# Layer norms of a four-layer graph network: squares by ScalarE in two halves of the tiles, and two elementwise steps of the last norm taken elsewhere

## The chip, the cores and the metric

One NeuronCore of a Trainium2 chip runs the whole network in one launch. The metric is device time in microseconds (us), the median over runs. TensorE is called PE in the profile, VectorE DVE, ScalarE ACT, GpSimd POOL and SyncE SP; they run unsynchronized, each through its own instruction stream, and meet at semaphores.

## The reference, cut to what matters

There are 3125 nodes with 128 features and 50000 edges. Each of the four layers takes the layer norm of x, clips it at zero, runs one graph layer on it and adds the result to x. The last layer (graph attention with 4 heads) ends in a layer norm of its own, with scale and shift:

```python
def _layernorm(x, axis=-1, eps=1e-05):
    m = jnp.mean(x, axis=axis, keepdims=True)
    v = jnp.var(x, axis=axis, keepdims=True)
    return (x - m) / jnp.sqrt(v + eps)

# layer 3 (attention), the end
combined = h_self + h_in.reshape(n, -1) + h_out.reshape(n, -1) + bias
mean = combined.mean(axis=-1, keepdims=True)
var = combined.var(axis=-1, keepdims=True)
normed = (combined - mean) * jax.lax.rsqrt(var + EPS_LN)
return normed * ln_gamma + ln_beta

# the frame around the four layers
h = jnp.maximum(_layernorm(x, axis=-1), 0.0)
x = x + _L0_gnn_ref(h, ...)
...
h = jnp.maximum(_layernorm(x, axis=-1), 0.0)
x = x + _L3_gnn_ref(h, ...)
```

## The kernel before, in words

**Tiling.** Nodes lie on the 128 partitions, in 25 tiles: `x`, `h` and `comb` (a view of `rdeg`) are 128 x 25 x 128 in f32, so a pass over all nodes is one instruction of 3200 elements a partition. `scr` is a view of the same size in `arena`.

**Stages.** First the edges are sorted and a dense matrix A of edge counts is built (up to about 850 us). Layers 0 to 2 each multiply the normed features by A (`dense_pe`, and `wide_pe` for the second step of layer 1) and then by weights. Layer 3 writes a table of projected rows to memory, GpSimd gathers 50000 padded edge rows from it (`stream_pool`), and in two directions d the kernel finds maxima (`top_*`), exponents (`guard_*`) and weighted sums (`weighted_*`). The last norm and the store of x end the program.

**The norms.** Norm 0 is GpSimd's (`first_norm`) and isn't touched. Norms 1, 2 and 3 stand ahead of layers 1, 2 and 3; norm 4 is the one that ends layer 3. They are `norm_dve(v, n, relu)`, L901 to L915. On DVE, one after the other: sum of each row (L904), mean (L905), subtraction of the mean (L906), square (L907), sum of the squares (L908). Then ScalarE takes the root (`norm_act`, L948) and DVE the reciprocal (L910) and the product (L912, or L915 in norm 4). `dve_link` adds a semaphore wait of DVE on its own last instruction. Nothing else of the layer runs meanwhile: PE waits for `h`. In norms 1 and 2 the split of `h` into three 16-bit parts (`split_dve`, `split_act`) stands between the norm and PE's product with A.

**The last norm.** Ahead of norm 4 DVE copies `comb` to `h` (L1605), and behind it stand the product with gamma (L1607), the addition of beta (L1608) and the addition to x (L1609), which releases the store.

**What sets the order.** Every engine's stream is in the order of the code; there is no scheduler. ScalarE's tables are loaded by an instruction that the compiler puts ahead of the first function that needs another set.

**Start of the attention.** DVE writes `h` for the table (L1571), then `comb` (L1573), then the indices that GpSimd waits for (L1577 to L1579), then digits and one-hot figures (L1580 to L1595, L1127, L1131). GpSimd's first gather waits for the indices and for both tables in memory.

Of the kernel before, what the change touches and what calls it, by code (L numbers as in the profile page):

```python
# [10 lines left out]
ALU = mybir.AluOpType  # L11
ACT = mybir.ActivationFunctionType
AX_X = mybir.AxisListType.X

P = 128
N_NODES, N_EDGES, D = 3125, 50000, 128
TILES = -(-N_NODES // P)
# [67 lines left out]
ROW = {"fc3": 0, "L2_self": 1, "L2_nei": 2, "L3_bias": 3, "gamma": 4, "beta": 5}  # L85
# [3 lines left out]
def linker(eng, sem):  # L89

    count = [0]

    def link(ins):
        count[0] += 1
        ins.then_inc(sem, 1)
        eng.wait_ge(sem, count[0])

    return link


def gnn_kernel(nc, edges, x_in, consts, steps, weights, bias_cols, bias_rows, attn, out):
    with ExitStack() as ctx:
        def sb(name, shape, dt=F32):
            return ctx.enter_context(nc.sbuf_tensor(name, shape, dt))

        def sem(name):
            return ctx.enter_context(nc.semaphore(name))
# [20 lines left out]
        brow = sb("brow", [P, ROWS, D])  # L128
# [5 lines left out]
        x = sb("x", [P, TILES, D])  # L134
        h = sb("h", [P, TILES, D])
        rdeg = sb("rdeg", [P, NP_])
        st = sb("st", [P, 8, TILES])
# [30 lines left out]
        scr = aggT.rearrange("p (t f) -> p t f", t=TILES)  # L168
# [72 lines left out]
        comb = rdeg[:, :].rearrange("p (t f) -> p t f", t=TILES)  # L241
# [52 lines left out]

        table = {n: sem(f"table_{n}") for n in ("att0", "att1")}
        digits_ready = sem("digits_ready")
        round_done = sem("round_done")
        scatters_begun = sem("scatters_begun")

        var_ready, std_ready, rstd_ready = sem("var_ready"), sem("std_ready"), sem("rstd_ready")  # L300
# [36 lines left out]
        dve_link = linker(nc.vector, dve_step)  # L337
# [432 lines left out]
        def split_need(t, n):  # L770
            def ready(k):
                for g, (c0, _) in enumerate(SPLITS):
                    if k == c0:
                        t.wait_ge(lo_ready, 1 + SPLIT_FROM[n] + g + 1)
            return ready
# [11 lines left out]
        def spread_src_dve(v):  # L787

            v.tensor_copy(spread, bc(src_deg[:, :], P)).then_inc(src_spread, 1)
            for m in range(DEG_PIECES):  # L790
                c = deg_piece(m)
                v.wait_ge(src_turned, m + 1)
                v.tensor_copy(rdeg[:, c], PS[:, SORT:SORT + c.stop - c.start]).then_inc(src_read, 1)
            v.wait_ge(src_read, DEG_PIECES)
# [39 lines left out]
        def h1_split_act(a):  # L834
            def hi(n):
                bank, _, p = h1_of(n)
                a.wait_ge(h1_turned, n + 1)
                a.copy(p[0], bank).then_inc(hi_ready, 1)

            def mid(n):  # L840
                _, left, p = h1_of(n)
                a.wait_ge(mid_rest, H1_MID + n + 1)
                a.copy(p[1], left).then_inc(mid_ready, 1)

            for n in range(TURNS + 1):
                if n < TURNS:
                    hi(n)
                if n:
                    mid(n - 1)
# [39 lines left out]
        def wide_dve(v):  # L889
            for b in range(BANDS):  # L890
                v.wait_ge(half_used, (b + 1) * TILES)
                for c in range(2):
# [2 lines left out]
                    v.tensor_tensor(agg2T[:, c, n].rearrange("p (q n) -> p q n", q=BQ), slot(c),  # L895
                                    rdeg[:, n].rearrange("p (q n) -> p q n", q=BQ), ALU.mult).then_inc(agg_ready, 1)

        def bc(a, n):
            return a.unsqueeze(2).to_broadcast([P, a.shape[1], n])

        def norm_dve(v, n, relu):  # L901

            src = x if relu else h
            dve_link(v.tensor_reduce(st[:, 0, :], src[:, :, :], AX_X, ALU.add))  # L904
            dve_link(v.tensor_scalar(st[:, 0, :], st[:, 0, :], 1.0 / D, None, ALU.mult))  # L905
            dve_link(v.tensor_tensor(h[:, :, :], src[:, :, :], bc(st[:, 0, :], D), ALU.subtract))  # L906
            dve_link(v.tensor_tensor(scr, h[:, :, :], h[:, :, :], ALU.mult))  # L907
            v.tensor_reduce(st[:, 1, :], scr, AX_X, ALU.add).then_inc(var_ready, 1)  # L908
            v.wait_ge(std_ready, n + 1)
            dve_link(v.reciprocal(st[:, 3, :], st[:, 2, :]))  # L910
            if relu:
                v.scalar_tensor_tensor(h[:, :, :], h[:, :, :], 0.0, bc(st[:, 3, :], D), ALU.max, ALU.mult) \  # L912
                    .then_inc(h_ready, 1)
            else:
                dve_link(v.tensor_tensor(h[:, :, :], h[:, :, :], bc(st[:, 3, :], D), ALU.mult))  # L915
# [28 lines left out]
            p.tensor_tensor(narrow[2], left, narrow[1], ALU.subtract).then_inc(lo_ready, 1)  # L944

        def norm_act(a, n):
            a.wait_ge(var_ready, n + 1)
            a.activation(st[:, 2, :], st[:, 1, :], ACT.Sqrt, bias=eps[:, 0:1], scale=1.0 / D).then_inc(std_ready, 1)  # L948

# [458 lines left out]
        def weighted_out_dve(v, d):  # L1408
            v.wait_ge(weighted_done, d + 1)
            n = TILES * HEADS  # L1410
            den = rden[:, 0, :]
            dve_link(v.tensor_reduce(den.rearrange("p (t h) -> p t h", h=HEADS), PS[:, DEG_COL:DEG_COL + SPLIT * n]
                                     .rearrange("p (t s h) -> p t h s", s=SPLIT, h=HEADS), AX_X, ALU.add))
            dve_link(v.tensor_scalar(den, den, 1e-8, None, ALU.add))
            dve_link(v.reciprocal(rden[:, 1, :], den))
            hv = h[:, :, :].rearrange("p t (h f) -> p (t h) f", h=HEADS)
            dve_link(v.tensor_tensor(hv, PS[:, 0:NP_].rearrange("p (n f) -> p n f", f=HD),
                                     rden[:, 1, :].unsqueeze(2).to_broadcast([P, n, HD]), ALU.mult))
            dve_link(v.tensor_tensor(comb, comb, h[:, :, :], ALU.add))
            v.nop().then_inc(den_ready, 1)  # L1420
# [65 lines left out]
        def _(v):  # L1486
# [21 lines left out]
            def row(a):  # L1508
                return a.unsqueeze(1).to_broadcast([P, TILES, D])
# [16 lines left out]
            dve_link(v.tensor_tensor(x[:, :, :], x[:, :, :], h[:, :, :], ALU.add))  # L1526

            norm_dve(v, 1, True)
            split_dve(v, 1)
            count_src_dve(v)  # L1530
# [10 lines left out]
            dve_link(v.tensor_tensor(x[:, :, :], x[:, :, :], h[:, :, :], ALU.add))  # L1541

            norm_dve(v, 2, True)
            split_dve(v, 2)
            spread_src_dve(v)
# [3 lines left out]
            dve_link(v.scalar_tensor_tensor(x[:, :, :], h[:, :, :], 0.0, x[:, :, :], ALU.max, ALU.add))  # L1549

            norm_dve(v, 3, True)
            v.wait_ge(hT_ready, HT_DONE + 1)
            v.wait_ge(score_summed, 1)
# [23 lines left out]
            dve_link(v.tensor_scalar(k0, back_i, 255, None, ALU.bitwise_and))  # L1577
            dve_link(v.tensor_scalar(key[:, 0, 0:CH[0]], k0, -1.0, None, ALU.add))
            v.tensor_scalar(k0, back_i, 8, None, ALU.arith_shift_right).then_inc(order0_ready, 1)  # L1579
            v.tensor_copy(figures, iota[:, 0:BASE])  # L1580
            for d in range(2):
                whole = digit_i[:, 0, 0:CH[d]]
# [16 lines left out]
            for d in range(2):  # L1599
# [2 lines left out]
                guard_dve(v, d)  # L1602
                weighted_dve(v, d)
                weighted_out_dve(v, d)
            dve_link(v.tensor_copy(h[:, :, :], comb))  # L1605
            norm_dve(v, 4, False)
            dve_link(v.tensor_tensor(h[:, :, :], h[:, :, :], row(brow[:, ROW["gamma"], :]), ALU.mult))  # L1607
            dve_link(v.tensor_tensor(h[:, :, :], h[:, :, :], row(brow[:, ROW["beta"], :]), ALU.add))  # L1608
            v.tensor_tensor(x[:, :, :], x[:, :, :], h[:, :, :], ALU.add).then_inc(x_final, 1)  # L1609

        @block.tensor
# [114 lines left out]
        def _(a):  # L1726
            a.wait_ge(wx_summed, 1)
            a.copy(Wx[:, :], PS[:, 6 * BANK:6 * BANK + SC]).then_inc(wx_ready, 1)
            norm_act(a, 0)
            a.wait_ge(placed, 1)  # L1730
            permute_act(a)
# [7 lines left out]
            a.wait_ge(sumsq_ready, 1)  # L1739
            a.activation(st[:, 7, :], st[:, 6, :], ACT.Sqrt).then_inc(len_ready, 1)  # L1740
            norm_act(a, 1)
            split_act(a, 1)
            ht_act(a, 1)
# [5 lines left out]
            act_link(a.activation(scr, scr, ACT.Exp, scale=-1.0))  # L1749
            a.activation(scr, scr, ACT.Ln, bias=1.0).then_inc(log_ready, 1)  # L1750
            norm_act(a, 2)
            split_act(a, 2)
            ht_act(a, 2)
# [85 lines left out]
```

## Time and profile before

| | us |
|---|---|
| median of 3 runs | 3366.75 |
| lowest, highest | 3361.63, 3368.27 |
| the profiled execution's own time | 3377.51 |
| its span, first to last instruction | 3375.7 |
| DVE busy in the span | 2277.1 (67%) |
| ACT busy | 835.0 (25%) |
| PE busy | 2190.7 (65%) |
| POOL busy | 1657.2 (49%) |

Time outside the span is 1.8 us. Busy shares are means over stages that different engines bound. In the four norms only DVE works for the layer; GpSimd still scatters sorted edges beside norms 1 and 2.

### The profile page before, as it was taken

To read this page: it belongs to the slowest core of one execution; us is meant where nothing else is said; L and a number is where in the kernel's file an instruction comes from. 1 tells how busy PE (TensorE), PEld (TensorE's weight loads), DVE (VectorE), ACT (ScalarE), POOL (GpSimd) and SP (SyncE) were. 2 spreads that over 40 slices of the span, in tenths; PEclk is the share of its full clock that TensorE was granted. 3 is DMA by queue.
4 is the path that set the end of the run, shared out by engine and by line. 5 is a ranking of instruction groups with operands and counts; after the bars stand their busy time and mean duration, and the time that the engine had idled before them with its cause. 6 is when DMAs were issued, how large, how long until landed. Compare 5 with 4: busy or idle time off the path is not lost.

```text
span 3375.7 us, 46741 instructions
## 1 busy us (share of the span) xinstructions
PE 2190.7 (65%) x12603; PEld 1296.6 (38%) x12659; DVE 2277.1 (67%) x3122; ACT 835.0 (25%) x1389; POOL 1657.2 (49%) x1455
## 2 busy tenths in 40 slices
PE   0488877777895989994963444434566665528562
PEld 0233455554452455542442111111456611118562
DVE  8999888898549720055132544444986799979777
ACT  0099433332001110022000111111344322206341
POOL 7400133332057777777104777777876777710000
PEclk9799999999997999997975555565569999955897
DMA  2000011110443524400725434435358733530452
GB/s 71 0 0 0 30 44 44 44 44 34 159 124 98 147 65 99 84 1 1 170 45 97 115 111 111 117 110 108 85 165 264 233 111 110 98 33 0 150 177 74
DMA packets 195115, 301.52 MB, mean 89 GB/s; under 512 B 120540, under 2 KB 133818, under 8 KB 194922
## 3 DMA queue, kind: packets, MB, share of 16 engines
q1 hardware_dynamic: 138986, 175.88, 16.7%
q0 software_dynamic: 40512, 62.87, 10.8%
q10 hardware_dynamic: 15552, 61.94, 6.0%
q8 instruction: 36, 0.59, 0.1%
q14 instruction: 29, 0.24, 0.0%
HBM read 191.65 MB, written 88.01 MB: 83 GB/s over the span
## 4 chain that ended last, share of the span: by engine, by line
PE 35%; POOL 19%; DVE 17%; issue 17%; DMA 6%; ACT 5%; ACTq 1%; DVEq 0%; SPq 0%; POOLq 0%; PEldq 0%
POOL arena L1304 19%; PE PS L537 11%; PE PS L698 9%; PE PS L883 6%; DMA arena<-T_att,idx 5%; ACT arena L513 4%; DVE arena L558 4%; PE PS L972 3%; PE PS L475 2%; PE PS L959 1%; DVE arena L1195 1%; DVE arena L373 1%; DVE arena L489 1%; DVE arena L566 1%; DMA T_att<-parts 1%
## 5 line engine op out<-in xcount | busy, mean ns | idle before, releaser
L1304 POOL DMA_INDIRECT arena<-T_att,idx x864 | 845.9, 979 | 323.1 <-issue 229.1
L537 PE MATMUL PS<-arena 128*128 128x400 f16 (+2 forms) x4320 | 780.6, 332 | 270.4 <-issue 112.1
L1139 DVE TENSOR_REDUCE arena<-PS 128x1024 f32 (+1 forms) x432 | 502.6, 1212 | 334.3 <-PE PS L1106 334.0
L537 PEld LDWEIGHTS PS<-arena 128*128 128x128 f16 (+2 forms) x4320 | 528.2, 158 | 513.6 <-issue 350.9
L1477 POOL DMA_INDIRECT order<-arena x400 | 514.2, 1285 | 249.4 <-issue 249.4
L558 DVE TENSOR_SCALAR arena<-arena 128x1600 f16<-128x1600 f16 x448 | 392.3, 919 | 63.1 <-PE PS L537 59.0
L1106 PE MATMUL PS<-arena,pick 128*128 128x512 bf16 x812 | 319.1, 493 | 154.1 <-DVE arena L1139 140.2
L698 PE MATMUL PS<-arena 128*128 128x512 f16 (+1 forms) x1575 | 318.1, 361 | 95.4 <-issue 82.1
L632 POOL TENSOR_TENSOR rdeg<-rdeg,arena 128x1600 f32<-128x1600 f32 x48 | 160.7, 3348 | 311.8 <-ACT arena L616 311.8
L1095 PE MATMUL PS<-ident_b,score_buf 128*32 128x128 bf16 x864 | 90.4, 268 | 314.8 <-ACT score_buf L1068 305.2
L698 PEld LDWEIGHTS PS<-arena 128*128 128x128 bf16 x1575 | 147.9, 99 | 261.6 <-issue 110.2
L1095 PEld LDWEIGHTS PS<-ident_b,score_buf 128*32 128x32 bf16 x864 | 66.9, 119 | 380.5 <-issue 305.2
L513 ACT ACTIVATE arena<-arena 125x128 f16<-125x128 f16 x600 | 186.1, 388 | 77.4 <-DVE arena L492 72.0
L1106 PEld LDWEIGHTS PS<-arena,pick 128*128 128x128 bf16 x864 | 61.9, 108 | 364.3 <-DVE arena L1139 319.8
L1351 DVE TENSOR_TENSOR arena<-PS,key 128x1024 f32<-128x1024 f32 x108 | 132.2, 1224 | 88.6 <-PE PS L537 86.2
L1241 PE MATMUL PS<-ident_b,arena 128*128 128x128 bf16 x864 | 109.4, 306 | 87.1 <-issue 66.5
L616 ACT CAST arena<-PS 128x1600 f16<-128x1600 f32 x50 | 74.6, 1492 | 345.1 <-PE PS L537 344.9
L1074 ACT COPY arena<-PS 32x1024 bf16<-32x1024 bf16 x108 | 107.8, 999 | 192.5 <-PE PS L1095 188.9
L883 PE MATMUL PS<-arena 128*128 128x400 f16 x800 | 147.1, 338 | 10.8 <-DVE arena L860 8.8
L972 PE MATMUL PS<-arena,W 128*128 (+1 forms) x384 | 136.7, 515 | 20.9 <-DVE arena L1002 10.2
L1273 ACT COPY arena<-PS 128x1024 bf16<-128x1024 bf16 x108 | 109.3, 1012 | 161.0 <-PE PS L1241 160.5
L1068 ACT COPY score_buf<-h 128x96 bf16 (+1 forms) x52 | 14.1, 271 | 535.1 <-POOL h L1313 535.1
(258 smaller groups left out, 2781.0 us busy)
## 6 DMA issues: line engine op xcount, KB each, us to landing
spill<-arena SPq DMA_DIRECT2D x108, 560.0 KB, 2.9
arena<-spill ACTq DMA_DIRECT2D x108, 560.0 KB, 3.8
arena<-A SPq DMA_DIRECT2D x50, 800.0 KB, 4.6
A<-arena SPq DMA_DIRECT2D x50, 400.0 KB, 2.4
arena<-A SPq DMA_DIRECT2D x50, 400.0 KB, 3.3
arena<-T_att,idx POOLq DMA_INDIRECT x864, 2.6
order<-arena POOLq DMA_INDIRECT x400
T_att<-h SPq DMA_DIRECT2D x2, 1600.0 KB, 13.9
```

What stands on the lines that cost most here:

```text
L513: last = a.activation(B0[:, g, j, k, :], eq0[:, g, j, :], ACT.Copy, scale=sort_v[:, 2 + k, c])
L537: return t.matmul(where, lhsT, rhs, start=False, stop=True, skip_group_check=True)
L558: v.tensor_scalar(oh_d[s], steps_h, dst_in[:, bass.ds(RING_D * i + s, 1)], None, ALU.is_equal) \
L632: p.tensor_tensor(at, at, stage[c % RING_A], ALU.add).then_inc(cell_counted, 1)
L698: last = t.matmul(PS[:, a0:a1], narrow[s][:, k, :], strips[g % RING][:, a0:a1], start=(k == 0 and s == 0), stop=(k == TILES - 1 and s == S ...
L883: last = t.matmul(PS[:, at:at + w], wide[c][s][:, k, :], halves[n % HALVES][:, q * w:(q + 1) * w], start=(k == 0 and s == 0), stop=(k == T ...
L972: last = t.matmul(o, wt(name, c * H1 + ob * P), rhs, start=(n == 0), stop=(n == len(terms) - 1))
L1095: last = t.transpose(bank[:, j * P:(j + 1) * P], score_buf[:, half, j, :], ident_b[:, :])
L1106: last = t.matmul(PS[:, hd * BANK:(hd + 1) * BANK], pick[:, hd, :], sT[:, s:s + QUAD, :].rearrange("p j e -> p (j e)"), start=True, stop=True)
L1139: v.tensor_reduce(cmax[d][:, u:u + 2, bass.ds(i * SLOTS + half * GROUP + q // 2 * QUAD, QUAD)], PS[:, u * BANK:(u + 2) * BANK].rearrange(" ...
L1304: p.indirect_dma_start(out=ring1[:, b, j, :], out_offset=None, in_=T_att[d][:, :], in_offset=bass.IndirectOffsetOnAxis(ap=idx[:, d, k:k + ...
L1477: p.indirect_dma_start(out=order0[:, :], out_offset=bass.IndirectOffsetOnAxis(ap=addr[:, j:j + 1], axis=0), in_=packed[:, j:j + 1], in_off ...
```

## The change

`norm_dve` subtracts the mean in two instructions, of 13 and of 12 tiles (`PARTS_T`), each of which increments `centred`. ScalarE waits for each and writes its squares to `scr` (increment of `squared`). DVE waits for each and sums it; the sum over a part is an instruction of its own, and the last increments `var_ready`. Norm 4 reads `comb` itself, so the copy to `h` goes. The addition of beta to x stands behind the indices at the start of the attention, and the one to `h` at the end goes.

```diff
@@ norm_dve
-            src = x if relu else h
+            src = x if relu else comb
             dve_link(v.tensor_reduce(st[:, 0, :], src[:, :, :], AX_X, ALU.add))
             dve_link(v.tensor_scalar(st[:, 0, :], st[:, 0, :], 1.0 / D, None, ALU.mult))
-            dve_link(v.tensor_tensor(h[:, :, :], src[:, :, :], bc(st[:, 0, :], D), ALU.subtract))
-            dve_link(v.tensor_tensor(scr, h[:, :, :], h[:, :, :], ALU.mult))
-            v.tensor_reduce(st[:, 1, :], scr, AX_X, ALU.add).then_inc(var_ready, 1)
+            for t in PARTS_T:
+                v.tensor_tensor(h[:, t, :], src[:, t, :], bc(st[:, 0, t], D), ALU.subtract).then_inc(centred, 1)
+            for k, t in enumerate(PARTS_T):
+                v.wait_ge(squared, 2 * (n - 1) + k + 1)
+                last = v.tensor_reduce(st[:, 1, t], scr[:, t, :], AX_X, ALU.add)
+            last.then_inc(var_ready, 1)
@@ norm_act
+            for k, t in enumerate(PARTS_T if n else ()):
+                a.wait_ge(centred, 2 * (n - 1) + k + 1)
+                a.activation(scr[:, t, :], h[:, t, :], ACT.Square).then_inc(squared, 1)
             a.wait_ge(var_ready, n + 1)
@@ start of the attention, behind the indices
+            v.tensor_tensor(x[:, :, :], x[:, :, :], row(brow[:, ROW["beta"], :]), ALU.add)
             v.tensor_copy(figures, iota[:, 0:BASE])
@@ the end
-            dve_link(v.tensor_copy(h[:, :, :], comb))
             norm_dve(v, 4, False)
             dve_link(v.tensor_tensor(h[:, :, :], h[:, :, :], row(brow[:, ROW["gamma"], :]), ALU.mult))
-            dve_link(v.tensor_tensor(h[:, :, :], h[:, :, :], row(brow[:, ROW["beta"], :]), ALU.add))
```

DVE's stream in norm 1, before and then after (`arena` is `scr` here):

```order
L904 TENSOR_REDUCE st<-x 128x25
L905 TENSOR_SCALAR st<-st 128x25
L906 TENSOR_TENSOR h<-x,st 128x3200
L907 TENSOR_TENSOR arena<-h 128x3200
L908 TENSOR_REDUCE st<-arena 128x25
L910 RECIPROCAL st<-st 128x25
```

```order
L907 TENSOR_REDUCE st<-x 128x25
L908 TENSOR_SCALAR st<-st 128x25
L910 TENSOR_TENSOR h<-x,st 128x1664
L910 TENSOR_TENSOR h<-x,st 128x1536
L913 TENSOR_REDUCE st<-arena 128x13
L913 TENSOR_REDUCE st<-arena 128x12
L916 RECIPROCAL st<-st 128x25
```

The square has left DVE, and the subtraction and the sum of squares are two instructions each. Lines of the changed kernel are some lines further down than those of before.

ScalarE's stream around norm 2, before and then after: absolute value, exponential and logarithm of layer 1's end, then the norm.

```order
L1749 ACTIVATE arena<-arena 128x3200
L1750 ACT_TABLE_LOAD
L1750 ACTIVATE arena<-arena 128x3200
L948 ACT_TABLE_LOAD
L948 ACTIVATE st<-st,eps 128x25
```

```order
L1757 ACTIVATE arena<-arena 128x3200
L1758 ACT_TABLE_LOAD
L1758 ACTIVATE arena<-arena 128x3200
L955 ACTIVATE arena<-h 128x1664
L955 ACTIVATE arena<-h 128x1536
L957 ACT_TABLE_LOAD
L957 ACTIVATE st<-st,eps 128x25
```

No load stands ahead of the squares; the root's load now comes behind them, here and in norm 4. In norms 1 and 3 no load is added.

DVE's stream at the start of the attention, after the change:

```order
L1588 TENSOR_SCALAR idx<-arena 128x416
L1589 TENSOR_TENSOR x<-x,brow 128x3200
L1590 CAST W<-cst 128x8
```

The middle row is new: x plus beta, behind the last instruction that GpSimd's gathers wait for.

## Rows read from the trace of the kernel before

**Rows 1.** The page: span, busy time by engine, the chain by engine.

```profile
span 3375.7 us, 46741 instructions
PE 2190.7 (65%) x12603; PEld 1296.6 (38%) x12659; DVE 2277.1 (67%) x3122; ACT 835.0 (25%) x1389; POOL 1657.2 (49%) x1455
PE 35%; POOL 19%; DVE 17%; issue 17%; DMA 6%; ACT 5%; ACTq 1%; DVEq 0%; SPq 0%; POOLq 0%; PEldq 0%
```

**Rows 2.** Timeline, norm 1: start us, length us, engine, line, [idle before <-releaser].

```profile
1024.19 3.49 DVE L904 TENSOR_REDUCE st<-x 128x25 f32<-128x3200 f32 x1
...
1028.21 3.49 DVE L906 TENSOR_TENSOR h<-x,st 128x3200 f32<-128x3200 f32 x1
...
1031.74 3.49 DVE L907 TENSOR_TENSOR arena<-h 128x3200 f32<-128x3200 f32 x1
...
1035.27 3.48 DVE L908 TENSOR_REDUCE st<-arena 128x25 f32<-128x3200 f32 x1
...
1038.79 0.32 ACT L948 ACTIVATE st<-st,eps 128x25 f32<-128x25 f32 x1 [22.24 <-DVE st L908]
1039.14 0.31 DVE L910 RECIPROCAL st<-st 128x25 f32<-128x25 f32 x1 [0.38 <-ACT st L948]
...
1047.75 6.57 PE L698 MATMUL PS<-arena 128*128 128x512 f16 x21 [37.91 <-issue]
```

**Rows 3.** Timeline, ScalarE from layer 1's end through norm 2.

```profile
1569.20 1.28 ACT L1750 ACT_TABLE_LOAD   x1
1570.49 2.87 ACT L1750 ACTIVATE arena<-arena 128x3200 f32<-128x3200 f32 x1
1573.38 1.28 ACT L948 ACT_TABLE_LOAD   x1
...
1595.04 0.32 ACT L948 ACTIVATE st<-st,eps 128x25 f32<-128x25 f32 x1 [20.38 <-DVE st L908]
```

**Rows 4.** Timeline, PE's first work behind norm 3.

```profile
1755.81 4.54 PE L952 MATMUL PS<-cst,h 128*128 128x128 f32 x25 [25.64 <-DVE h L912]
```

**Rows 5.** Timeline, smaller pieces in the split behind norm 1.

```profile
1044.09 2.36 DVE L754 TENSOR_TENSOR arena<-h,arena 128x1024 f32<-128x1024 f32 x2 [1.11 <-ACT arena L734]
...
1046.29 1.15 ACT L734 CAST arena<-h 128x1152 bf16<-128x1152 f32 x1
...
1047.56 1.35 DVE L754 TENSOR_TENSOR arena<-h,arena 128x1152 f32<-128x1152 f32 x1
```

**Rows 6.** Timeline, start of the attention: DVE's preparations, the first gather, the first consumer.

```profile
1798.03 0.38 DVE L1579 TENSOR_SCALAR idx<-arena 128x416 int32<-128x416 int32 x1
...
1805.39 0.18 DVE L1131 TENSOR_TENSOR score_buf<-W 128x32 bf16<-128x32 bf16 x1
1813.13 1.01 POOL L1304 DMA_INDIRECT arena<-T_att,idx  x1 [37.09 <-DMA T_att<-parts]
...
1833.24 0.27 ACT L1068 COPY score_buf<-h 128x96 bf16<-128x96 bf16 x1 [70.03 <-POOL h L1313]
```

**Rows 7.** Timeline, the program's end.

```profile
3323.78 1.28 ACT L948 ACT_TABLE_LOAD   x1
...
3335.94 1.83 DVE L1605 COPY h<-rdeg 128x3200 f32<-128x3200 f32 x1
...
3359.85 3.49 DVE L1608 TENSOR_TENSOR h<-h,brow 128x3200 f32<-128x3200 f32 x1
3363.38 3.49 DVE L1609 TENSOR_TENSOR x<-x,h 128x3200 f32<-128x3200 f32 x1
3366.90 0.41 SPq L1456 DMA_DIRECT2D out<-x  x1
```

**Rows 8.** Timeline, PE in two successive rounds of the last weighted sums.

```profile
3175.57 2.05 PE L537 MATMUL PS<-arena 128*128 128x128 f32 x16 [0.96 <-issue]
...
3178.71 2.05 PE L537 MATMUL PS<-arena 128*128 128x128 f32 x16 [0.91 <-issue]
```

**Rows 9.** Windows: stretch, its us, busy us of five engines, PE's granted clock, DMA.

```profile
3170.00:3180.00 10.00, 6.87 (x76) 6.57 (x75) 7.21 (x7) 4.58 (x8) 0.00 (x0) 1.00 0.58 177
```

More of the change, by code:

```diff
@@ L296, in gnn_kernel @@
         digits_ready = sem("digits_ready")
+        centred, squared, senders_summed = sem("centred"), sem("squared"), sem("senders_summed")
         round_done = sem("round_done")
@@ L896, in wide_dve @@
                                     rdeg[:, n].rearrange("p (q n) -> p q n", q=BQ), ALU.mult).then_inc(agg_ready, 1)
+        PARTS_T = (slice(0, TILES // 2 + 1), slice(TILES // 2 + 1, TILES))
         def bc(a, n):
```

## The prediction

> **What bounds the kernel now.** I first read the page: DVE is busy 67% of the span and PE 65%, and the chain that ended last is PE 35%, GpSimd 19%, DVE 17% [rows 1]. No engine bounds the whole, so a change is worth what it is worth in its own stage. Then the timeline of a norm. In norm 1 DVE runs one full-size instruction after the other, each starting 0.03 to 0.04 us after the last (1028.21 + 3.49, then 1031.74); PE stands idle and starts only at 1047.75, after 37.91 us [rows 2]. Norm 2 stands alone in the same way: ScalarE had been idle 20.38 us when the sum of squares released it [rows 3]. In norm 3 PE, idle for 25.64 us, is released by DVE's product L912 directly [rows 4]. At the end nothing runs but DVE, and the store is issued 0.03 us after its last addition [rows 7]. So all four norms lie on the path, DVE alone makes them, and the time of each is a sum of its instructions.
>
> GpSimd also works beside norms 1 and 2 (the scatters of the sort), but nothing waits for it there: its first gather waits for the table in memory [rows 6].
>
> **The cost of the smaller instructions.** The trace shows no DVE pass over 13 or 12 tiles (1664 or 1536 elements a partition). It has 3.49 us for 3200 elements [rows 2] and 1.35 us for 1152 [rows 5]: 1.045 ns an element and 0.15 us fixed. That gives 1.89 us for 13 tiles and 1.75 for 12. The same line is taken for the sums, since L908 with 3.48 costs what L907 does. Two instructions that don't wait for each other overlap by 0.07 us: a pass of 1024 is 1.22 by that line, and two together took 2.36 [rows 5].
>
> ScalarE's square from `h` to `scr` isn't shown either. The nearest rows are its logarithm over the same 3200 elements, 2.87 us [rows 3], and its cast of 1152 from `h`, 1.15 us [rows 5]: 0.84 ns an element and 0.18 fixed. So 1.58 us for 13 tiles and 1.47 for 12.
>
> A handoff from DVE to ScalarE costs 0.04 us: L908 ends at 1038.75, the root starts at 1038.79. Back it costs 0.03: the root ends at 1039.11, the reciprocal starts at 1039.14 [rows 2].
>
> **Part 1, the squares, four times.** Before, from the start of the subtraction to the start of the root: 1038.79 - 1028.21 = 10.58 us [rows 2]. After, with the subtraction of the first part at 0:
> - first subtraction ends at 1.89, the second runs from 1.82 to 3.57;
> - first square from 1.93 to 3.51, beside the second subtraction; second square from 3.61 to 5.08;
> - first sum from 3.60 (DVE is free at 3.57, its square was done at 3.51) to 5.49; second sum from 5.42 to 7.17, its square long done;
> - root at 7.21.
>
> That is 3.37 us a norm: the whole square (3.53 with its gap) less the second fixed cost of two DVE passes, part of which the overlap returns. Neither square is on the path; what hides the second is the first sum, with 0.34 us to spare (5.42 against 5.08). Four norms give 13.5 us. The bounds: at best the square goes and nothing comes, 3.53 a norm, 14.1. At worst neither overlap happens (0.14) and each of DVE's two waits for a square costs 0.38, the whole idle time that DVE shows around the root [rows 2], although 0.32 of it was the root itself: 3.37 - 0.14 - 0.76 = 2.5 a norm, 10 in all. I take 13.5, near the upper end, since two of the rows (the handoffs of 0.04 and 0.03) are the very kind of wait that is added.
>
> Queued behind DVE's two waits are only the norm's own later steps. On ScalarE nothing else stands there: in norms 1 and 2 the casts that need the finished `h`, in norm 3 the copy behind PE's transposes.
>
> **The root's table.** Before norms 2 and 4 ScalarE loads the root's table while idle (1573.38, and 3323.78 during the last weighted sums) [rows 3, 7]. Now the load follows the second square: from 5.08 to 6.37, and the root isn't wanted until 7.21. The second sum hides it with 0.84 us to spare. Were that cover gone, it would cost its 1.28.
>
> The trace shows a switch at 1.29 us from the start of the load to the start of the logarithm, with 0.02 us ahead of it [rows 3]. The Trainium skill, "ScalarE: Activation LUTs", section "What ACT_TABLE_LOAD costs", puts a drain of about 1380 ns on top, 2.66 us for every switch. By that rule, an estimate from the page, the root would be ready at about 7.74 and norms 2 and 4 would each lose 0.5 us; the trace doesn't agree with it, so my sum leaves it out.
>
> **Part 2, the copy ahead of norm 4.** It goes with its gap: 1.83 + 0.03 = 1.86 us [rows 7]. The sum L904 and the subtraction then read `comb`, an f32 tile of the same size in the same memory, so they keep 3.49. Bounds 1.8 and 1.9.
>
> **Part 3, beta.** At the end one addition with its gap goes: 3363.38 - 3359.85 = 3.53 us [rows 7]. At the start of the attention the same instruction is added behind the indices (1798.03 + 0.38 = 1798.41). It pushes DVE's remaining preparations back by 3.5 us, from an end at 1805.57 to 1809.1. The first gather waits for the table, until 1813.13, and not for DVE; the first consumer of the figures comes with ScalarE's copy at 1833.24 [rows 6]. The cover is 24 us, so I cost it at 0; without it the price would be the 3.5 us. GpSimd issues nothing in that stretch for DVE to disturb.
>
> **The sum.** 13.5 + 1.86 + 3.53 = 18.9 us. The profiled execution took 3377.51 (3375.7 of span and 1.8 around it), so its like would take 3358.6. The median shown is 10.8 us under the profiled execution; the terms don't depend on that difference, and 3366.75 - 18.9 = 3347.9. I predict 3348.
>
> **Rivals.**
> 1. *Only the tail is kept.* What norms 1 to 3 give (10.1 us) is absorbed at a gate that doesn't move with them: a strip of A not yet landed, or the gather stage. Then 3.37 + 1.86 + 3.53 = 8.8 us remain, 3358. The same total, near enough, comes if the squares take twice as long beside a busy DVE: second square done at 8.1 instead of 5.1, 0.8 us gained a norm, 8.6 in all. For the gate: gathers wait on memory. Against it: behind norms 1 and 2 the product starts when the split is done, and the gathers start when the table lands, which is itself released by DVE's and PE's chain from norm 3. Against slow squares: ScalarE's 1152-element cast had DVE beside it and lies on the same line as the lone 2.87.
> 2. *Beta isn't free.* DVE's preparations hold somebody. Then 15.4 us, 3351.4. Against it the 24 us of cover.
> 3. *The switch with its drain.* The root's table is ready only at about 7.7, because the load can't follow a busy ScalarE at once. From a ready time 0.5 us late in two norms the gain is 17.9, 3348.9. For it: here the load stands behind a square, with the root wanted soon after. Against it: in norm 2 the present load began 0.02 us after the logarithm and ended 1.29 later. The page that states this is named above.
> 4. *Slower: PE loses its clock in the last weighted sums.* Everything reaches that stage earlier than before by 10 us, and the granted clock there could come late. The granted clock is 1.00 (2.4 GHz) in this stretch [rows 9], a round takes 3.14 us, and its 16 matmuls 2.05 [rows 8]. At half the clock these would be some 4.1 (an estimate, twice 2.05), so a round would lengthen by 2.05. Of its 56 rounds 9 at half clock cancel the gain, and 13 make the kernel slower by over 0.2%; all 56 would cost 115 us. Against it: the work that comes before the stage is the same instruction by instruction, and the three runs shown lie within 6.6 us.
>
> That the change doesn't do what it says I leave without a chance of its own: the streams show the square gone from DVE.
>
> **Chances.** Forecast (16 to 21 us gained) 0.78; drain 0.04; beta not free 0.05; only the tail or slow squares 0.09; PE's clock 0.04. A measurement of this kernel tells about 0.2% (6.7 us) from no change. The first three are faster beyond that (0.87), of the fourth two thirds (0.06, the rest falls within as its 8.8 us is near the bound), and the clock case is slower with 0.03 and within with 0.01. Faster 0.93, same 0.04, slower 0.03.
>
> The range: the sum's own bounds are 10 + 1.8 + 3.53 = 15.3 and 14.1 + 1.9 + 3.53 = 19.5, so 3347 to 3351; the runs of before lie from 5 us under to 1.5 above their median, and a new set of runs has the same spread. The fourth case ends at 3358. I take 3340 to 3358.
>
> **What would show it.** In norms 1 to 4: subtractions of about 1.89 and 1.75 us, squares of 1.58 and 1.47 on ScalarE, the root 7.2 us after the first subtraction's start instead of 10.6. DVE idle ahead of the first sum for about 0.03 us and ahead of the second for none. In norms 2 and 4 a load of 1.28 us that ends before the second sum. DVE's last preparation of the attention 3.5 us later against the table's write, and the first gather still released by the table. From the last addition to comb to the store's issue 31.0 - 3.4 - 1.9 - 3.5 = 22.2 us (before: 3366.90 - 3335.94 = 31.0). What would prove me wrong: a wait of DVE on `squared` of over 0.3 us, full-size passes that got longer, or a stage between 1060 and 3320 that changed its length by more than some 3 us.

## The result, and the profile after

The changed kernel takes 3346.68 us (median of 5 runs, 3344.86 to 3349.36), the kernel before 3366.34 in the same comparison (5 runs, 3361.63 to 3368.27). The ratio is 0.9947, 95% interval 0.9937 to 0.9958: 19.7 us less. The forecast was 3348, 18.9 less.

The page of the changed kernel, beside [rows 1] (its profiled execution took 3349.36 us):

```profile
span 3347.6 us, 46752 instructions
PE 2186.4 (65%) x12603; PEld 1297.7 (39%) x12659; DVE 2262.1 (68%) x3125; ACT 846.9 (25%) x1397; POOL 1645.1 (49%) x1455
PE 35%; POOL 19%; issue 16%; DVE 16%; DMA 6%; ACT 5%; ACTq 1%; DVEq 0%; SPq 0%; POOLq 0%; PEldq 0%
```

DVE has 15 us less work and ScalarE 12 more: in each of the four norms the two squares of 1.59 and 1.48 us. The shares hardly tell of the change. The timeline of norm 1 does (start us, length us, engine, line, [idle before <-releaser]; lines are those of the changed kernel), against [rows 2]:

```profile
1023.72 3.49 DVE L907 TENSOR_REDUCE st<-x 128x25 f32<-128x3200 f32 x1
...
1027.74 3.56 DVE L910 TENSOR_TENSOR h<-x,st 128x1664 f32<-128x1664 f32 x2
1029.66 3.15 ACT L955 ACTIVATE arena<-h 128x1664 f32<-128x1664 f32 x2 [13.59 <-DVE h L910]
1031.29 3.54 DVE L913 TENSOR_REDUCE st<-arena 128x13 f32<-128x1664 f32 x2
1034.87 0.32 ACT L957 ACTIVATE st<-st,eps 128x25 f32<-128x25 f32 x1 [2.05 <-DVE st L913]
1035.21 0.31 DVE L916 RECIPROCAL st<-st 128x25 f32<-128x25 f32 x1 [0.38 <-ACT st L957]
...
1043.83 6.43 PE L699 MATMUL PS<-arena 128*128 128x512 f16 x20 [34.46 <-issue]
```

A row with x2 holds both parts. From the subtraction to the root it is 1034.87 - 1027.74 = 7.13 us, where it was 10.58. Neither sum has an idle time ahead of it, and DVE goes straight from subtraction to sums. Even so the first sum is not free of ScalarE: it starts 0.03 to 0.04 us after the end of the first square (1029.66 + 1.59 = 1031.25, with the length that a later run shows apart), just as the second subtraction ends (1027.74 + 3.56 = 1031.30). PE starts 20.11 us after the norm's first sum, where it started 23.56 us after it (1047.75 - 1024.19).

ScalarE in norm 2, against [rows 3]:

```profile
1580.50 3.56 DVE L910 TENSOR_TENSOR h<-x,st 128x1664 f32<-128x1664 f32 x2
1582.42 3.15 ACT L955 ACTIVATE arena<-h 128x1664 f32<-128x1664 f32 x2 [13.03 <-DVE h L910]
...
1585.59 1.28 ACT L957 ACT_TABLE_LOAD   x1
1587.63 0.32 ACT L957 ACTIVATE st<-st,eps 128x25 f32<-128x25 f32 x1 [0.75 <-DVE st L913]
```

The load follows the second square at once and is over 0.75 us before the root starts. The start of the attention, against [rows 6], and the end, against [rows 7]:

```profile
1787.41 3.48 DVE L1589 TENSOR_TENSOR x<-x,brow 128x3200 f32<-128x3200 f32 x1
...
1797.89 0.18 DVE L1140 TENSOR_TENSOR score_buf<-W 128x32 bf16<-128x32 bf16 x1
1799.56 1.01 POOL L1313 DMA_INDIRECT arena<-T_att,idx  x1 [34.42 <-DMA T_att<-parts]
...
1819.62 0.27 ACT L1077 COPY score_buf<-h 128x96 bf16<-128x96 bf16 x1 [67.32 <-POOL h L1322]
```

```profile
3312.96 3.49 DVE L1428 TENSOR_TENSOR rdeg<-rdeg,h 128x3200 f32<-128x3200 f32 x1
3316.60 3.49 DVE L907 TENSOR_REDUCE st<-rdeg 128x25 f32<-128x3200 f32 x1
...
3331.68 3.49 DVE L1616 TENSOR_TENSOR h<-h,brow 128x3200 f32<-128x3200 f32 x1
3335.21 3.49 DVE L1617 TENSOR_TENSOR x<-x,h 128x3200 f32<-128x3200 f32 x1
3338.73 0.41 SPq L1465 DMA_DIRECT2D out<-x  x1
```

From the first sum of norm 4 to the store's issue it is 22.13 us; with the copy and beta it was 3366.90 - 3335.94 = 30.96. So the tail gives 8.83.

The two profiled executions differ by 28 us, not by 19.7. Cut at instructions that both have, the stretches are as follows; the columns marked "again" and "third" are later profiles of the same two kernels.

| stretch, us | before | before, again | after | after, third |
|---|---|---|---|---|
| start to norm 1's first sum | 1024.2 | 1021.2 | 1023.7 | 1024.0 |
| to norm 2's | 556.3 | 556.3 | 552.8 | 552.8 |
| to norm 3's | 156.8 | 156.8 | 153.3 | 153.3 |
| to the first gather | 75.9 | 73.2 | 69.8 | 69.8 |
| to the last gather | 1163.3 | 1158.4 | 1157.6 | 1155.2 |
| to the last scaling of the sums | 352.4 | 352.7 | 352.2 | 352.2 |
| to the store's issue | 38.1 | 38.1 | 29.3 | 29.3 |

In these four profiles the changed stretches repeat to 0.1 us, but for the write of the table ahead of the first gather. Between before again and after third the four stretches with a norm give 3.5 + 3.5 + 3.5 + 8.8 = 19.3 us, and that is the measured gain within its interval.

### The profile page after: what moved, and what is told of

Read it like the earlier page. It is cut to its first block, busy times and chain, and to the rows that moved or that the text cites. A ratio compares the mean times of both kernels' runs of the same rounds, so it can differ in the third digit from the quotient of the medians.

```text
span 3347.6 us, 46752 instructions
## 1 busy us (share of the span) xinstructions
PE 2186.4 (65%) x12603; PEld 1297.7 (39%) x12659; DVE 2262.1 (68%) x3125; ACT 846.9 (25%) x1397; POOL 1645.1 (49%) x1455
## 4 chain that ended last, share of the span: by engine, by line
PE 35%; POOL 19%; issue 16%; DVE 16%; DMA 6%; ACT 5%; ACTq 1%; DVEq 0%; SPq 0%; POOLq 0%; PEldq 0%
POOL arena L1313 18%; PE PS L538 11%; PE PS L699 9%; PE PS L884 6%; DMA arena<-T_att,idx 5%; ACT arena L514 4%; DVE arena L559 4%; PE PS L981 3%; PE PS L476 2%; DVE arena L1204 1%; PE PS L968 1%; DVE arena L374 1%; DVE arena L490 1%; POOL W L1322 1%; DVE arena L567 1%
## 5 line engine op out<-in xcount | busy, mean ns | idle before, releaser
L1486 POOL DMA_INDIRECT order<-arena x400 | 504.8, 1262 | 246.5 <-issue 246.5
L1104 PEld LDWEIGHTS PS<-ident_b,score_buf 128*32 128x32 bf16 x864 | 66.6, 119 | 371.9 <-issue 299.6
```

Of the source, the lines that this page charges most:

```text
L1104: last = t.transpose(bank[:, j * P:(j + 1) * P], score_buf[:, half, j, :], ident_b[:, :])
L1486: p.indirect_dma_start(out=order0[:, :], out_offset=bass.IndirectOffsetOnAxis(ap=addr[:, j:j + 1], axis=0), in_=packed[:, j:j + 1], in_off ...
```

## The experiments

**The changed kernel again.** No edit.

> The changed kernel once more, as it is. Theory (the gain is the 18.9 to 19.2 us of the norms' own instructions, and what the two profiles show beyond it, 2.7 us in the table's write and 5.8 us in the attention, is what one execution differs from the next): median 19 to 20 us under the kernel before, and in the new profile the stretch from the first gather to norm 4 anywhere from 1513 to 1520 us. Rival (the attention runs shorter because it starts earlier): that stretch is again 1513 to 1514 us.

Measured: 3347.3 us (3343.65 to 3349.15), before 3366.42 (21 runs); ratio 0.9943 (0.9929 to 0.9956): 19.1 less, in the expected 19 to 20. The stretch that the expectation speaks of, from the first gather to the addition ahead of norm 4 (1519.2 in the first profile of before, 1513.4 in that of after), took 1510.7 us, less than either had said; in the third profile it is 1510.9. That left open whether the kernel before is slower there, which its own second profile was to settle.

**The kernel before, profiled again.** No edit.

> The kernel before, profiled once more. Its first profile had 1163 us from the first gather to the last and 75.8 us from norm 3's first sum to the first gather; the changed kernel, its parts alone and its variants have 1154 to 1158, and 69.7 to 70.6 with the shorter norm (72.8 without). Theory (one execution's own scatter): now some 1155 to 1158 and 73 to 74. Rival (the kernel before is slower there, from where its gathers lie in time): again about 1163 and 75.8.

Measured: 3367.39 us (one run). 73.2 us from norm 3 to the first gather, 1158.4 over the gathers. So the first profile of before had 2.7 and 4.9 us of its own there, and most of the extra 8.6 us between the two first profiles is no gain of the change. Whether the 0.7 to 3.4 us that are left over the gathers (1158.4 against 1157.6, 1155.0 and 1155.2 in three profiles of the changed kernel) mean anything can't be said from single profiles.

**Only the squares.** The copy and the late beta put back:

```diff
-            src = x if relu else comb
+            src = x if relu else h
...
-            v.tensor_tensor(x[:, :, :], x[:, :, :], row(brow[:, ROW["beta"], :]), ALU.add)
...
+            dve_link(v.tensor_copy(h[:, :, :], comb))
             norm_dve(v, 4, False)
...
+            dve_link(v.tensor_tensor(h[:, :, :], h[:, :, :], row(brow[:, ROW["beta"], :]), ALU.add))
```

> Only the squares by ScalarE in two halves; the copy ahead of norm 4 and the late addition of beta as before. Theory: 4 x 3.45 = 13.8 us under the kernel before. Rival (the gain sits in the tail and in the attention, the norms 1 to 3 pass nothing on): 3.5 us under it.

Measured: 3350.84 us (3349.03 to 3352.57), ratio 0.9953 (0.994 to 0.9967), 15.6 less, interval 11 to 20. The theory's 13.8 lies in it, and the rival's 3.5 is out: norms 1 to 3 pass their gain on. The stretch from norm 3 to the first gather is 69.7 us here, without the early addition of beta, and 69.8 with it.

**Only the tail.** The kernel before without copy and late beta, with the early one.

> Only the copy gone and beta added at the start of the attention; squares by DVE as before. Theory: 1.86 + 3.53 = 5.4 us under the kernel before, to be seen in the tail of the profile. Rival (beta at the start of the attention holds somebody): 1.9 us.

Measured: 3357.18 us (11 runs, 3352.58 to 3364.89), ratio 0.9974 (0.9965 to 0.9983), 9.2 less, interval 5.7 to 11.8. The rival's 1.9 is out; the theory's 5.4 lies just below the interval. In the profile the last stretch takes 32.7 us where it took 38.1, which is the 5.4. Its other stretches are like those of the kernel before but for the gathers, 1154.9. Where the rest comes from stays open. The two halves of the change do not add up either: 15.6 and 9.2 make 24.8, where the whole gives 19.7. Three variants gain more than their rows say (the squares alone 1.8 us more, this one 3.8, the next one 3.5), the changed kernel at most 0.5, and no run tells why.

**One part instead of two.**

```diff
-        PARTS_T = (slice(0, TILES // 2 + 1), slice(TILES // 2 + 1, TILES))
+        PARTS_T = (slice(0, TILES),)
```

The counts that the two engines wait for follow the number of parts.

> The changed kernel with one part of 25 tiles in place of two: subtraction 3.49, handoff 0.04, square 2.87, handoff 0.03, sum 3.48, so the root starts 9.95 us after the subtraction. Theory: 2.8 us a norm lost, 11.3 us over the changed kernel, 8 under the one before; the sum still hides the root's table. Rival (most of the gain is that ScalarE squares faster than DVE, not that it does so beside it): within 3 us of the changed kernel.

Measured: 3355.02 us (11 runs, 3351.38 to 3362.37), ratio 0.9971 (0.9962 to 0.998), 11.4 under before (6.7 to 12.8) and 7.7 over the changed kernel. Norm 1 in its timeline:

```profile
1024.39 3.49 DVE L910 TENSOR_TENSOR h<-x,st 128x3200 f32<-128x3200 f32 x1
1027.91 2.87 ACT L955 ACTIVATE arena<-h 128x3200 f32<-128x3200 f32 x1 [15.19 <-DVE h L910]
1030.82 3.48 DVE L913 TENSOR_REDUCE st<-arena 128x25 f32<-128x3200 f32 x1 [2.94 <-ACT arena L955]
1034.34 0.32 ACT L957 ACTIVATE st<-st,eps 128x25 f32<-128x25 f32 x1 [3.55 <-DVE st L913]
```

DVE waits 2.94 us, and the root comes after 9.95, the sum of the expectation. ScalarE's faster square is worth 0.63 us a norm; the halves are worth the other 2.82. By the rows four norms lose 11.3 to the changed kernel; the medians say 7.7, with intervals that allow both. The rival (within 3 us of the changed kernel) is out by the rows of the norm.

**The second square twice.**

```diff
             for k, t in enumerate(PARTS_T if n else ()):
                 a.wait_ge(centred, 2 * (n - 1) + k + 1)
+                if k:
+                    act_link(a.activation(scr[:, t, :], h[:, t, :], ACT.Square))
                 a.activation(scr[:, t, :], h[:, t, :], ACT.Square).then_inc(squared, 1)
```

> The changed kernel with ScalarE squaring the second part twice, the second time behind a wait on the first: 1.5 us more ahead of the second sum. Theory: the second square ends at 6.6 us after the subtraction's start instead of 5.1, the second sum could start at 5.3, so DVE waits 1.3 us and the root comes 8.4 us after the subtraction's start instead of 7.1; in norms 2 and 4 the root's table (6.6 to 7.9) is still hidden. Rival (ScalarE isn't near the path): root at 7.1 as before.

This kernel, the next one, the one with ten more passes and the first run of the last experiment ran on another chip, on which the kernel before took 4086.03 us; their profiles reach the first gather at the usual time, so only rows of the norms and of the attention's start are read from them. Norm 1:

```profile
1024.23 3.56 DVE L910 TENSOR_TENSOR h<-x,st 128x1664 f32<-128x1664 f32 x2
1026.15 1.59 ACT L957 ACTIVATE arena<-h 128x1664 f32<-128x1664 f32 x1 [13.60 <-DVE h L910]
...
1027.78 1.89 DVE L913 TENSOR_REDUCE st<-arena 128x13 f32<-128x1664 f32 x1
...
1029.33 1.48 ACT L957 ACTIVATE arena<-h 128x1536 f32<-128x1536 f32 x1
1030.85 1.75 DVE L913 TENSOR_REDUCE st<-arena 128x12 f32<-128x1536 f32 x1 [1.19 <-ACT arena L957]
1032.63 0.32 ACT L959 ACTIVATE st<-st,eps 128x25 f32<-128x25 f32 x1 [1.82 <-DVE st L913]
```

1.51 us more of ScalarE cost 8.40 - 7.13 = 1.27. The cover behind the second square is thus 0.24 us, where 0.34 was forecast: the forecast left out the handoff from ScalarE back to DVE (0.03), and the second sum could start sooner than it said. The rows also show the parts' lengths apart: 1.59 and 1.48 for the squares, 1.89 and 1.75 for the sums. And the first sum starts 0.04 us after the first square's end (1026.15 + 1.59 = 1027.74), while the second subtraction ends at 1024.23 + 3.56 = 1027.79. So the first square, which no run lengthened, has no cover at all.

**A table switch that is exposed.**

```diff
+            if n:
+                a.activation(st[:, 5, :], st[:, 3, :] if n > 1 else st[:, 0, :], ACT.Exp, scale=0.0)
             a.wait_ge(var_ready, n + 1)
```

> The changed kernel with an exponential of 25 elements a partition, whose result nobody reads, on ScalarE between squares and root. In norms 1 to 3 two table loads then follow the squares. Theory (a switch costs its 1.28 us load and nothing more): exponential's table 5.1 to 6.4, exponential to 6.7, root's table to 8.0, so the root starts 8.0 us after the subtraction's start, 0.85 later than in the changed kernel. Rival (each switch has a drain of 1.38 us on top): root at 10.7. Norm 4 has only the root's load, as before: 7.1 by the theory, 7.8 by the rival.

Norm 1:

```profile
1025.04 3.56 DVE L910 TENSOR_TENSOR h<-x,st 128x1664 f32<-128x1664 f32 x2
...
1030.14 1.28 ACT L957 ACT_TABLE_LOAD   x1
1031.43 0.22 ACT L957 ACTIVATE st<-st 128x25 f32<-128x25 f32 x1
1031.66 1.28 ACT L959 ACT_TABLE_LOAD   x1
1032.95 0.32 ACT L959 ACTIVATE st<-st,eps 128x25 f32<-128x25 f32 x1
```

The root comes 7.91 us after the subtraction, here and in norm 2; 8.0 by the theory and 10.7 by the rival. Two switches back to back cost their 1.28 us and 0.01 to 0.02 around each; a drain of 1.38 us is not there. In norm 4, with the root's load alone, the root comes after 7.13, as in the changed kernel, and not after the rival's 7.8.

**Ten, and five, more passes behind beta.**

```diff
             v.tensor_tensor(x[:, :, :], x[:, :, :], row(brow[:, ROW["beta"], :]), ALU.add)
+            for _ in range(10):
+                dve_link(v.tensor_tensor(h_spare, comb, comb, ALU.add))
```

> The changed kernel with ten more full-size additions on DVE behind the one of beta, into memory that nobody reads, 10 x 3.52 = 35.2 us. In the changed kernel DVE's preparations end at 1798.1 and ScalarE's copy comes at 1819.6. Theory: 21.5 us of them are hidden and the first transposes of the attention start about 14 us later than ScalarE's first copy would allow; the gathers start no later, and run on until their ring of three is full, so that most of the delay is caught up later: less than 14 us in the time. Rival (DVE's work here holds the gathers' start): the first gather itself comes 35 us later.

> The changed kernel with five more additions on DVE behind the one of beta (17.6 us). With ten, DVE was busy until 1826 us, the first gather wasn't later, but the first eight gathers of a tile group took longer while DVE worked, and ScalarE's first copy came at 1838.4 instead of 1819.6. Theory (DVE's passes slow GpSimd's issuing of gathers while both run): DVE ends at about 1809 and the preparations at 1816, the copy comes some 5 to 7 us later than in the changed kernel, at about 1826. Rival (the copy waited for DVE's preparations): copy at 1819.6, since they end before it.

With ten passes:

```profile
1791.16 35.21 DVE L1593 TENSOR_TENSOR arena<-rdeg 128x3200 f32<-128x3200 f32 x10
```

```profile
1799.70 2.89 POOL L1315 DMA_INDIRECT arena<-T_att,idx  x1 [34.20 <-DMA T_att<-parts]
1802.89 3.17 POOL L1315 DMA_INDIRECT arena<-T_att,idx  x1 [0.30 <-issue]
1806.37 3.20 POOL L1315 DMA_INDIRECT arena<-T_att,idx  x1 [0.30 <-issue]
...
1827.50 1.21 POOL L1315 DMA_INDIRECT arena<-T_att,idx  x1 [0.30 <-issue]
...
1832.14 0.94 POOL L1315 DMA_INDIRECT arena<-T_att,idx  x1 [0.30 <-issue]
...
1838.38 0.27 ACT L1079 COPY score_buf<-h 128x96 bf16<-128x96 bf16 x1 [85.72 <-issue]
```

With five, the row of GpSimd's third gather and the copy:

```profile
1799.06 3.20 POOL L1315 DMA_INDIRECT arena<-T_att,idx  x1 [0.30 <-issue]
...
1819.70 0.27 ACT L1079 COPY score_buf<-h 128x96 bf16<-128x96 bf16 x1 [74.33 <-POOL h L1324]
```

Both theories of the first of these fell. The first gather is no later. But while DVE works, each gather takes 2.9 to 3.2 us instead of 0.94, one for each of DVE's passes (both some 3.5 us apart), and ScalarE's first copy comes 38.7 us after the first gather (1838.38 - 1799.70), where the changed kernel has 20.1. With five passes DVE is done at 1801.44 and its preparations at 1808.9; the gathers beside its passes take 2.92, 3.17 and 3.20, and the copy comes at 1819.70, 27.3 us after the first gather (1792.36), 7.3 more than in the changed kernel. That is the effect of about 5 to 7 us that the slowed gathers were to have: the three beside the passes are together 6.4 us longer than the changed kernel's first three, and the next three, beside DVE's preparations (1.21, 1.15 and 1.38), 0.9. The copy is released by GpSimd's own cast behind the sixteenth gather; the copy's absolute time, which I had put at 1826, means nothing, as this execution reached norm 1 some 6 us sooner. The rival is out, since the preparations end well before the copy. The times were 4091.9 beside 4086.03 of before, and 3350.14, one run each. The runs with the doubled square and with the exposed switch, one each on the same chip as the ten passes, took 4077.23 and 4079.76, 12 to 15 us less than the ten passes did. The one with five lies just above the fifteen runs of the changed kernel (3343.65 to 3349.82), and its stretch over the gathers is 1164.8 us, 7 to 10 more than in that kernel's three profiles; this is one profile, and the kernel before had 1163.3 there once for no known reason.

**The idea carried on.** The product of norms 1 to 3 in the three parts of the split, the split in another order, PE's transposes of norm 3 part by part, the last addition and the store in two:

```diff
...
+            product(0)
+            product(1)
             mid(0)
-            mid(1)
+            product(2)
             lo(0)
-            mid(2)
+            mid(1)
             lo(1)
+            mid(2)
             lo(2)
...
-            t.wait_ge(h_ready, 4)
-            transposes_pe(t, h_tile, hT_summed)
+            for g, (c0, c1) in enumerate(SPLITS):
+                t.wait_ge(h_part, 6 + g + 1)
+                for k in range(c0, c1):
+                    last = t.transpose(PS[:, k * P:(k + 1) * P], h_tile(k), ident)
+            last.then_inc(hT_summed, 1)
```

> The changed kernel, and the same idea carried on: the norms' product in the three parts of the split, so that ScalarE's casts (norms 1 and 2) and PE's transposes (norm 3) start behind the first part, the split's steps reordered to lo(0) first, the last addition to x in two parts, and the store in two. Theory: PE's product starts some 2.2 us earlier in norms 1 and 2, the transposes end some 2 us earlier in norm 3, the store some 1.5 us: about 8 us under the changed kernel. Rival (PE's product with A then waits for lo(1) and lo(2), and a store is as long from its last issue): 3 us or less.

It ran on the other chip: 4061.2 us (4055.27 to 4065.61) against 4086.03, ratio 0.994 (0.9927 to 0.9954), without the changed kernel beside it. So both were run together:

> The changed kernel once more, as the partner of the next run on the same chip. All theories: 19 to 20 us under the kernel before.

> The version with the product, the split, the last addition and the store in parts, beside the changed kernel on one chip. From its first profile, against that of the changed kernel, from the norm's first sum: PE's second strip 1.6 us sooner in norm 1 and 3.1 in norm 2, the transposes' end 1.6 sooner in norm 3, the store's last issue 1.7 sooner. Theory: all four are on the path, 6 to 8 us under the changed kernel. Rival (one or two of them are taken back behind the stretch that was read): 3 us or less.

Measured: the changed kernel 3347.16 (3344.76 to 3349.82), this one 3337.08 (3334.28 to 3340.3), ratios to before 0.9944 (0.9931 to 0.9958) and 0.9915 (0.9901 to 0.9929). It is 10.1 us faster than the changed kernel, more than the 6 to 8 expected. Norm 1:

```profile
1035.92 2.36 DVE L923 SCALAR_TENSOR_TENSOR h<-h,st 128x1024 f32<-128x1024 f32 x2
1037.18 2.18 ACT L735 CAST arena<-h 128x1024 bf16<-128x1024 f32 x2 [1.64 <-DVE h L923]
...
1041.98 3.25 PE L699 MATMUL PS<-arena 128*128 128x512 f16 x8 [32.27 <-issue]
```

PE starts 17.91 us after the first sum (from 1024.07), 2.2 less, in norm 2 as well. Cut as in the table above, the stretches are 549.5, 150.5, 66.6, 1155.2, 352.8 and 27.7 us, the last to the issue of the store's first half. Against after third the three with a norm at their head give 3.3, 2.8 and 3.2, where the expectation had 1.6, 3.1 and 1.6. The end gives 1.6: the store's first half is issued that much sooner, its second half no sooner than the whole was. The excess is not certain: these are single profiles, and with five passes behind beta, whose code is the changed kernel's up to there, the first of the stretches took 551.8 where that kernel has 552.8.

## Why the prediction was right

**What bounds.** That DVE alone makes the norms and everything behind shifts with them held: 3.5 us a norm in the stretches behind norms 1 to 3. Elsewhere the stretches changed by no more than profiles of one kernel do. By the prediction's own sign of being wrong, a stage that changes its length by over some 3 us, the first pair of profiles would have spoken against it (1163.3 and 1157.6 us over the gathers); the second profile of before takes most of that back and leaves 0.7 to 3.4 us open.

**The squares.** 3.37 us a norm were forecast, 3.45 measured. The 0.08 is mostly the first sum's start: forecast at 3.60, a gap after the second subtraction's end, measured at 3.55; the rest is in the length of the two sums, 3.54 for 3.57. The mechanism was wrong in one point here, at no cost to the number. "Neither square is on the path" holds for the second alone. The first sum starts 0.03 to 0.04 us after the first square's end, in all four norms, where two passes with no wait between them overlap by 0.08 (1.89 + 1.75 against 3.56). An estimate from these rows: the wait for the first square costs some 0.07 us a norm, and a slower first square would add all of its excess. The sizes from two rows each (1.89 and 1.75; 1.58 and 1.47) came out within 0.01 on ScalarE and, where they were seen apart, on DVE. Rival 1, as slow squares or as a gate that doesn't move, is out by the rows and by the run with the squares alone.

**The root's table.** Forecast from 5.08 to 6.37 after the subtraction, measured from 5.09 to 6.37, and the root follows at 7.13, sooner than the 7.7 of rival 3. It is out by the norm-2 rows and more clearly by the exposed switches.

**Copy and beta.** 1.86 + 3.53 with norm 4's own 3.45 make 8.84; the tail shows 8.83.

**Beta at the start of the attention.** The cost, nothing, was right, and so was the remark that GpSimd issues nothing beside the added pass; the cover was not. I put it at 24 us, up to ScalarE's first copy. It ends with the first gather: a two-input pass of DVE that runs beside the gathers cost GpSimd 1.9 to 2.3 us for each gather that it met. The changed kernel's pass ends at 1790.9, 8.7 us before the first gather; DVE's preparations end 1.5 us before it. Behind that point the price is not zero, as five passes showed.

**PE's clock.** Rival 4 had no trace: the last scaling comes 352.2 to 352.7 us after the last gather in all four profiles of the table, and the granted clock was 1.00 (2.4 GHz) from 3150 to 3290 us in each.

**The sum.** 18.9 forecast, 19.7 measured, 19.3 by the stretches: 0.3 of the difference is the four times 0.08, the rest is within what the runs tell.

## What to carry to other kernels

A pass that one engine hands to another in halves disappears from the path only if each half is shorter than the step of the first engine beside it; here the first half was just short enough. The halves were worth 2.8 of 3.45 us, the faster engine 0.6. Where a chain stands alone between stages, price each of its full-size passes and look for those that can be done at any other time (beta), then pass parts on to the next consumer too, which gave another 10 us. Ask of work that is moved elsewhere not only who waits for its result, but also what runs beside it. Read a difference of two profiles only in the stretches that the change touches, and profile a kernel twice before explaining the rest.

## What the runs showed of the hardware

- DVE's two-input f32 passes hold up GpSimd's indirect DMA instructions, and not the other way round: each gather took 2.9 to 3.2 us instead of 0.94 while `tensor_tensor` passes ran, and the passes kept their 3.49 us. A gather that had started beside a pass ended 0.8 to 0.9 us after that pass did, beside the next one. Beside DVE's sum of norm 1 (L908) the scatters kept their 1.19 us:

```profile
1033.07 3.23 POOL L1477 DMA_INDIRECT order<-arena  x1 [0.30 <-issue]
1036.60 1.19 POOL L1477 DMA_INDIRECT order<-arena  x1 [0.30 <-issue]
1038.09 1.19 POOL L1477 DMA_INDIRECT order<-arena  x1 [0.30 <-issue]
```

  These are of the kernel before; the first started beside the square (L907) and ended 1.1 us after it. The Trainium skill, "SBUF — State Buffer", section "Who interferes with whom", says that a DVE instruction with two SBUF inputs contends with a GpSimd instruction that reads SBUF and that `tensor_reduce` never does. The trace agrees with both, for DMA instructions that read their indices from there.
- The same program took 4086.03 us on one chip and 3366 on another. In a profile there (the exposed switch), DVE idled up to 27.5 us between two maxima of the attention's first direction and ScalarE up to 43.7, together with PE. The first direction's maxima took 1268 us from the first to the last, where the changed kernel has 519; the second direction's took 270 and 289. The cause is open.
- Executions differ by up to 8 us before norm 1 is reached (1016.4 to 1024.3 us in fourteen profiles), while the stretches from norm 1 to norm 3 repeat to 0.1 us among profiles of the kernel before and among those of the changed one. That is not so everywhere: with the same code in it, the stretch from norm 1 to norm 2 took 551.8 with five passes, and the version in parts took 552.4 on the chip of 4086 us and 549.5 on the other.
